# Five maxima over the partitions in a feed forward: by transpose and row maximum in place of a GpSimd reduction

## The chip, the cores and the metric

The kernel runs on one core of a Trainium2 chip. The metric is the device time of one execution in microseconds (us). PE is TensorE, DVE VectorE, ACT ScalarE, POOL GpSimd, SP SyncE, which issues most of the DMAs.

## The reference, cut to what matters

A decoder layer: self attention, cross attention, and a quantised feed forward, each followed by a layer norm. Four sequences of 1024 tokens are 4096 rows of 512. The change is in the feed forward:

```python
def act_qdq(x):
    scale = jnp.maximum(jnp.max(jnp.abs(x)) / qmax, 1e-12)     # one maximum over the whole tensor
    return jnp.clip(jnp.round(x / scale), -qmax - 1.0, qmax) * scale
x = act_qdq(x)
up = act_qdq(x @ lpbq_dequant(w_up).T)
gate = act_qdq(x @ lpbq_dequant(w_gate).T)
sig = fixed_qdq_u16(jax.nn.sigmoid(gate))
gate = act_qdq(gate * sig)
o = act_qdq(gate * up)
return o @ lpbq_dequant(w_down).T
```

Each `act_qdq` needs the largest absolute value of a whole tensor before one element of it can be rounded.

## The kernel before

The layer is a string of phases: preparation, self attention, projection, cross attention, and then the feed forward, which is `second_norm_phase`, `gate_phase`, `up_phase`, `product_phase` and `down_phase`. A phase is one block in which each engine has its own instruction stream, written out by hand with semaphores; a block ends when all engines have arrived and the last stores have landed, and then POOL clears the phase's semaphores and all engines meet again (`Kit.clear`). So no work of a phase begins before the one ahead of it is over on all engines.

- `second_norm_phase`: POOL adds (L1369), DVE normalises, ACT stores. DVE leaves in `pmax_x` a maximum for each partition.
- `gate_phase`: DVE rounds the input by `scale_x`, PE transposes it (L113) with the f32 identity `idf` and multiplies (L128), ACT evicts, DVE takes row maxima (L1550). POOL issues 26 DMAs of weights (L1524) and has nothing else.
- `up_phase`: PE multiplies 96 tiles of 128x512. For each ACT rounds the gate (`v_r`, L1648), takes the sigmoid (`v_s`, L1660) and evicts (L1669); POOL scales the sigmoid (`v_t`, L1693) and multiplies (`v_h`, L1682); DVE does the rest, among it `v_t` in place (L1724) and two row maxima.
- `product_phase`: 48 tiles of 128x1024 in rounds of four buffers. SP loads `j_h` (L1759) when DVE's product has freed the buffer; ACT rounds twice (L1801, L1804), POOL subtracts (L1813), DVE multiplies (L1828) and takes the row maximum (L1831). The first 24 tiles have their other factor and their result in SBUF (`rows`); the others load it and store the result.
- `down_phase`: ACT and DVE round and split, PE multiplies (L1927), DVE adds and normalises. POOL has nothing in it.

Between them stand the quantisers: `qx` (input), `qg` (gate), `quh` (up and h, two maxima) and the product's, which multiplies the maximum by a unit. Each is a block of its own. POOL reduces a 128x1 tile of maxima over the partitions (L1434, L1848), and DVE makes `scale` and `inverse` of it (L1440, L1442), which every partition needs. Nothing else runs in these blocks.

Of the kernel before, what the change touches and what calls it, by code (L numbers as in the profile page):

```python
# [15 lines left out]
F32 = mybir.dt.float32  # L16
# [3 lines left out]
ALU = mybir.AluOpType  # L20
ACT = mybir.ActivationFunctionType
AX = mybir.AxisListType
RMAX = bass.bass_isa.ReduceOp.max
ds = bass.ds

P = 128
# [1393 lines left out]
                dve.wait_ge(done, 1)  # L1420


def quantisers(nc, name, of):


    with ExitStack() as ctx:
        kit = Kit(nc, ctx)
        amax = [kit.sb(f"{name}_amax{j}", [P, 1], F32) for j in range(len(of))]
        reduced, steps = kit.sem(f"{name}_reduced"), kit.sem(f"{name}_steps")
        with nc.Block() as block:  # L1430
            @block.gpsimd
            def _(pool):
                for j, (pmax, scale, inverse) in enumerate(of):
                    nc.gpsimd.partition_all_reduce(amax[j][:], pmax[:], P, RMAX).then_inc(reduced, 1)  # L1434

            @block.vector
            def _(dve):
                for j, (pmax, scale, inverse) in enumerate(of):
                    dve.wait_ge(reduced, j + 1)
                    nc.vector.tensor_scalar(scale[:], amax[j][:], 1.0 / QMAX, 1e-12, ALU.mult, ALU.max).then_inc(steps, 1)  # L1440
                    dve.wait_ge(steps, 2 * j + 1)
                    nc.vector.reciprocal(inverse[:], scale[:]).then_inc(steps, 1)  # L1442
                    dve.wait_ge(steps, 2 * j + 2)
# [392 lines left out]
                dve.wait_ge(done, 1)  # L1836


def product_quantiser(nc, omax, sh, su, so, iso):

    with ExitStack() as ctx:
        kit = Kit(nc, ctx)
        amax, unit, inv = (kit.sb(f"qo_{n}", [P, 1], F32) for n in ("amax", "unit", "inv"))
        reduced, steps = kit.sem("qo_reduced"), kit.sem("qo_steps")
        with nc.Block() as block:
            @block.gpsimd
            def _(pool):
                nc.gpsimd.partition_all_reduce(amax[:], omax[:], P, RMAX).then_inc(reduced, 1)  # L1848

            @block.vector  # L1850
            def _(dve):
                nc.vector.tensor_tensor(unit[:], sh[:], su[:], ALU.mult).then_inc(steps, 1)
                dve.wait_ge(reduced, 1)
                dve.wait_ge(steps, 1)
                nc.vector.tensor_tensor(amax[:], amax[:], unit[:], ALU.mult).then_inc(steps, 1)
                dve.wait_ge(steps, 2)
                nc.vector.tensor_scalar(so[:], amax[:], 1.0 / QMAX, 1e-12, ALU.mult, ALU.max).then_inc(steps, 1)
                dve.wait_ge(steps, 3)
                nc.vector.reciprocal(inv[:], so[:]).then_inc(steps, 1)
                dve.wait_ge(steps, 4)  # L1860
                nc.vector.tensor_tensor(iso[:], inv[:], unit[:], ALU.mult).then_inc(steps, 1)
                dve.wait_ge(steps, 5)
# [125 lines left out]
def feed_forward(nc, c, attn2, x1_dram, w_dram, scratch, out):  # L1988

    x2_dram = scratch("scr_x2", [T, D], F32)  # L1990
    x_dram = [scratch(f"scr_xq_{n}", [NG, P, KT * GT], F16) for n in ("hi", "lo")]
    gate_dram, up_dram, h_dram, o_dram = (scratch(f"scr_{n}", [FT, P, T], F32) for n in ("gate", "up", "h", "o"))
    with ExitStack() as ctx:
        kit = Kit(nc, ctx)
        names = ("x", "gate", "up", "h", "o")
        pmax, scale, inverse = ({n: kit.sb(f"{k}_{n}", [P, 1], F32) for n in names} for k in ("pmax", "scale", "inverse"))
        of = lambda n: (pmax[n], scale[n], inverse[n])
        wd = [kit.sb(f"wd_{n}", [P, FT, D], F16) for n in ("hi", "lo")]

        res = kit.sb("rows", [P, RES * T], F32)  # L2000
        x2 = res[:, 0:T // P * D]
        with ExitStack() as up_scope:
            wu = [Kit(nc, up_scope).sb(f"wu_{n}", [P, FT, KT, P], F16) for n in ("hi", "lo")]
            with ExitStack() as gate_scope:
                wg = [Kit(nc, gate_scope).sb(f"wg_{n}", [P, FT, KT, P], F16) for n in ("hi", "lo")]
                tiles = lambda w, m: [(w[j][:].rearrange("p t k n -> p t (k n)"), w_dram[j][m * FT:(m + 1) * FT].rearrange("t p n -> p t n"))
                                      for j in range(2)]

                down_tiles = [(wd[j][:, k * KT:(k + 1) * KT, r * P:(r + 1) * P], w_dram[j][2 * FT + r * 3 + k].rearrange("p (q n) -> p q n", n=P))
                              for j in range(2) for r in range(KT) for k in range(3)]  # L2010
                second_norm_phase(nc, attn2, x1_dram, x2, x2_dram, pmax["x"], tiles(wg, 0))
                quantisers(nc, "qx", [of("x")])
                gate_phase(nc, c, x2, scale["x"], inverse["x"], wg, gate_dram, x_dram, pmax["gate"], tiles(wu, 1) + down_tiles)
            quantisers(nc, "qg", [of("gate")])
            up_phase(nc, x_dram, scale["x"], wu, gate_dram, scale["gate"], inverse["gate"], up_dram, res, h_dram,
                     pmax["up"], pmax["h"])
        quantisers(nc, "quh", [of("up"), of("h")])
        product_phase(nc, h_dram, up_dram, res, inverse["h"], inverse["up"], o_dram, pmax["o"])
        product_quantiser(nc, pmax["o"], scale["h"], scale["up"], scale["o"], inverse["o"])
        down_phase(nc, o_dram, res, scale["o"], inverse["o"], wd, x2_dram, out)  # L2020


def decoder_layer(nc, x, context, mask, Wq, bq, Wk, bk, Wv, bv, Wf, bf, w_gate, w_up, w_down, out):
    x = x.rearrange("b s d -> (b s) d")
    context = context.rearrange("b s d -> (b s) d")
    mask = mask.rearrange("b o q k -> (b o q) k")
    out = out.rearrange("b s d -> (b s) d")

    def scratch(name, shape, dt):
        return nc.dram_tensor(name, shape, dt).ap()  # L2030

    qk_dram = [scratch(f"scr_{n}", [B, D, S], F16) for n in ("q_hi", "q_lo", "k_hi", "k_lo")]
    q2_dram = [scratch(f"scr_q2_{n}", [B, D, S], F16) for n in ("hi", "lo")]
    k2_dram = [scratch(f"scr_k2_{n}", [B, D, S], F16) for n in ("hi", "lo")]
    v_dram, v2_dram = scratch("scr_v", [B * H, P, ST, VW], F16), scratch("scr_v2", [B * H, P, ST, VW], F16)
    mb_dram, nm_dram = scratch("scr_mb", [T, S], BF16), scratch("scr_nm", [B, S, S], F16)
    w_dram = [scratch(f"scr_w_{n}", [3 * FT, P, KT * P], F16) for n in ("hi", "lo")]
    place_dram = scratch("scr_place", [H, S], F16)
    attn, attn2, x1_dram = (scratch(n, [T, D], F32) for n in ("scr_attn", "scr_attn2", "scr_x1"))

    with ExitStack() as ctx:
        c = make_identities(nc, Kit(nc, ctx))
        preparation_phase(nc, c, x, Wq, bq, Wk, bk, Wv, bv, qk_dram, v_dram, context, k2_dram, v2_dram,
                          mask, mb_dram, nm_dram, (w_gate, w_up, w_down), w_dram)
        attention_phase(nc, c, "self", True, qk_dram[0:2], qk_dram[2:4], v_dram, attn, place_dram=place_dram)
        projection_phase(nc, c, attn, x, Wf, bf, x1_dram, q2_dram)
        attention_phase(nc, c, "cross", False, q2_dram, k2_dram, v2_dram, attn2, mb_dram, nm_dram)
        feed_forward(nc, c, attn2, x1_dram, w_dram, scratch, out)
# [21 lines left out]
```

## Time and profile before

| | us |
|---|---|
| median of 3 runs | 3291.91 (3290.72 to 3293.62) |
| the profiled execution, its own time | 3299.95 |
| its span | 3298.2 |

| engine | busy us | share of the span |
|---|---|---|
| PE | 2655.0 | 80% |
| DVE | 2426.0 | 74% |
| ACT | 1751.6 | 53% |
| POOL | 2008.6 | 61% |

The shares are means over phases with different limits. Times in the rows below are microseconds from the start of the span. An engine's idle time stands in brackets, with what ended it; "issue" means that the profile shows nothing that the engine waited for.

### The profile page before, as it was taken

The numbers are of one execution on the slowest core, as the hardware profiler recorded it, in microseconds if no ns is written. First come the engines' busy times: TensorE is split into PE (matmuls) and PEld (weight loads), VectorE is DVE, ScalarE is ACT, GpSimd is POOL, SyncE is SP. The second block draws the span as 40 slices with busy tenths as digits, with TensorE's granted clock in tenths as the row PEclk, the third lists the DMA queues.
The fourth block names the chain that finished last, engine by engine and source line by source line (L and its number), as shares of the span: only waits on it lengthen the run. The fifth ranks groups of instructions, "written<-read, shape, count | busy, mean of one in ns | idle before, by whom it ended". The sixth has DMA issues, their size and how long they took to land. (4 is left out here: it accounts for less than half of the span.)

```text
span 3298.2 us, 79323 instructions
## 1 busy us (share of the span) xinstructions
PE 2655.0 (80%) x24114; PEld 1432.6 (43%) x24114; DVE 2426.0 (74%) x4633; ACT 1751.6 (53%) x3234; POOL 2008.6 (61%) x1479
## 2 busy tenths in 40 slices
PE   6888748888886969999999999904998899301999
PEld 3444325555553525555555555502444333100444
DVE  7778757777774777888888888765433899785776
ACT  2433327777775526666666666601332666585333
POOL 2334369999997309999999999943000566441000
PEclk9999969999998979999999999956999999755999
DMA  7999934444445651131131221176333677587332
GB/s 242 298 304 289 308 101 130 136 131 129 131 140 179 231 189 36 46 96 51 43 98 45 66 81 48 48 270 207 137 119 146 205 249 244 184 307 303 122 121 83
DMA packets 339452, 518.73 MB, mean 157 GB/s; under 512 B 36165, under 2 KB 169029, under 8 KB 339354
## 3 DMA queue, kind: packets, MB, share of 16 engines
q1 hardware_dynamic: 331066, 499.72, 47.4%
q0 software_dynamic: 2752, 9.44, 0.9%
q10 hardware_dynamic: 5536, 8.40, 0.7%
q8 instruction: 45, 0.74, 0.1%
q14 instruction: 53, 0.43, 0.0%
HBM read 278.56 MB, written 202.67 MB: 146 GB/s over the span
## 5 line engine op out<-in xcount | busy, mean ns | idle before, releaser
L1085 POOL TENSOR_TENSOR cross_plo<-cross_p 128x1024 f16<-128x1024 f32 x448 | 906.4, 2056 | 73.8 <-ACT cross_p L923 69.7
L923 ACT ACTIVATE cross_p<-cross_st 128x512 f32<-128x512 f32 x1024 | 556.1, 595 | 289.3 <-PE cross_st L857 289.3
L998 DVE CUSTOM_DVE_ANT_0 cross_junk<-cross_sc,cross_mb 128x1024 bf16<-128x1024 f32 x512 | 619.3, 1220 | 110.1 <-PE cross_sc L818 98.3
L1085 POOL TENSOR_TENSOR self_plo<-self_p 128x1024 f16<-128x1024 f32 (+7 forms) x512 | 576.7, 1161 | 20.4 <-ACT self_p L923 20.1
L923 ACT ACTIVATE self_p<-self_st,self_strip 128x512 f32<-128x512 f32 (+3 forms) x768 | 415.3, 582 | 149.1 <-PE self_st L855 118.2
L998 DVE CUSTOM_DVE_ANT_0 self_junk<-self_sc,self_strip 128x1024 bf16<-128x1024 f32 (+7 forms) x512 | 371.3, 753 | 141.9 <-PE self_sc L818 136.0
L852 PE MATMUL cross_st<-cross_qa,cross_ka 97*128 97x512 f16 x1024 | 390.6, 381 | 2.3 <-ACT cross_p L923 1.9
L857 PE MATMUL cross_st<-cross_nm,idbig 128*128 128x512 f16 x1024 | 390.0, 381 | 0.0
L818 PE MATMUL cross_sc<-cross_ka,cross_qa 96*128 96x512 f16 x1024 | 311.3, 386 | 21.9 <-DMA cross_ka<-scr_k_hi 16.6
L1927 PE MATMUL d_acc<-wd_hi,d_oh 128*128 128x512 f16 x384 | 146.7, 382 | 204.4 <-DVE d_ol L1965 204.4
L880 PEld LDWEIGHTS cross_o<-cross_vh,cross_p 128*128 128x128 bf16 x4096 | 270.1, 97 | 75.1 <-issue 21.8
L880 PE MATMUL cross_o<-cross_vh,cross_p 128*128 128x65 f16 x4096 | 297.4, 191 | 4.7 <-POOL cross_plo L1085 4.3
L881 PE MATMUL cross_o<-cross_vh,cross_plo 128*128 128x33 f16 x4096 | 291.1, 179 | 0.0
L852 PE MATMUL self_st<-self_qa,self_ka 98*128 98x512 f16 (+3 forms) x768 | 244.4, 334 | 48.7 <-ACT self_p L923 44.2
L881 PEld LDWEIGHTS cross_o<-cross_vh,cross_plo 128*128 128x128 f16 x4096 | 249.1, 96 | 53.9
L818 PE MATMUL self_sc<-self_ka,self_qa 96*128 96x512 f16 (+3 forms) x768 | 212.8, 334 | 53.9 <-DVE self_strips L972 27.9
L880 PE MATMUL self_o<-self_vh,self_p 128*128 128x65 f16 x2304 | 199.2, 192 | 40.4 <-DVE self_osum L1021 19.9
L510 POOL TENSOR_TENSOR qk_out<-y,qk_out 128x512 f16<-128x512 f32 x64 | 74.1, 1158 | 203.0 <-DVE qk_out L475 203.0
L880 PEld LDWEIGHTS self_o<-self_vh,self_p 128*128 128x128 bf16 x2304 | 163.1, 98 | 74.9 <-issue 43.6
L881 PE MATMUL self_o<-self_vh,self_plo 128*128 128x33 f16 x2304 | 191.8, 179 | 0.0
L1550 DVE TENSOR_REDUCE gt_tmax<-gt_y 128x512 f32 x96 | 65.8, 685 | 162.1 <-ACT gt_y L1515 162.1
L128 PE MATMUL v_acc<-v_xh,wu_hi 128*128 128x512 f16 x384 | 148.9, 388 | 33.9 <-ACT rows L1669 21.7
(241 smaller groups left out, 6007.2 us busy)
## 6 DMA issues: line engine op xcount, KB each, us to landing
self_strip<-self_strips SPq DMA_DIRECT2D x68, 516.0 KB, 3.2
v_g<-scr_gate SPq DMA_DIRECT2D x97, 256.0 KB, 3.8
scr_gate<-gt_y SPq DMA_DIRECT2D x96, 256.0 KB, 2.0
scr_h<-v_h SPq DMA_DIRECT2D x96, 256.0 KB, 2.4
j_h<-scr_h SPq DMA_DIRECT2D x48, 512.0 KB, 6.0
m<-in_mask_Bx1xSxS_ik SPq DMA_DIRECT2D x34, 512.0 KB, 7.6
d_o<-scr_o SPq DMA_DIRECT2D x9, 1536.0 KB
scr_up<-v_y SPq DMA_DIRECT2D x48, 256.0 KB, 3.5
```

Of the source, the lines that this page charges most:

```text
L128: mm = nc.tensor.matmul(out, a, b, start=(n == 0), stop=(n == len(terms) - 1))
L510: nc.gpsimd.tensor_tensor(qk[:, n // 4, 1, n % 4], y32[:, n % 4], qk[:, n // 4, 0, n % 4], ALU.subtract).then_inc(l_done, 1)
L818: mm = nc.tensor.matmul(sc[slot % 2][:, k - k0:k - k0 + w], qa[j][0:3 * HD, qt * P:(qt + 1) * P], ka[j][0:3 * HD, k:k + w], start=True, st ...
L852: mm = nc.tensor.matmul(out[:, 0:w], lhs, qa[j][0:KR, q0:q1], start=True, stop=causal)
L857: mm = nc.tensor.matmul(out[:, 0:w], c["idbig"][:], nm[kt][:, q0:q1], start=False, stop=True)
L880: nc.tensor.matmul(out[:, qt % 4, :], high[:, q], vh[n % NQK][:, kt, :], start=first, stop=False, skip_group_check=True)
L881: mm = nc.tensor.matmul(out[:, qt % 4, 0:HD + 1], plo[u % NPR][:, q], vh[n % NQK][:, kt, 0:HD + 1], start=False, stop=last_kt, skip_group_ ...
L923: nc.scalar.activation(p32[u % NPR][:, q0:q1], stp[cc % 2][:, 0:q1 - q0], ACT.Exp, bias=bias, scale=SM).then_inc(expd, 1)
L998: nc.vector.tensor_tensor_reduce(junk[slot % 2][:, 0:w], sc[slot % 2][:, 0:w], bias, 1.0, -3e38, ALU.add, ALU.max, qmax[n % 2][:, qt:qt + ...
L1085: nc.gpsimd.tensor_tensor(plo[u % NPR][:, q], p32[u % NPR][:, q], high[:, q], ALU.subtract).then_inc(lo_g, 1)
L1550: nc.vector.tensor_reduce(tmax[:, ds(g * FT + o, 1)], y[o % NY][:], AX.X, ALU.max, apply_absolute_value=True).then_inc(maxed, 1)
L1927: mm = nc.tensor.matmul(acc[tt % 2][:], a[:, k, t], b[:, k, :], start=(n == 0), stop=(n == 3 * FT - 1))
```

## The change

The reduction on POOL is replaced by three steps. DVE copies the 128x1 maxima over 128 columns (`wide`), PE transposes that tile into PSUM (`turned`), so that each partition has all 128 maxima in its row, and DVE takes the maximum of the row. In `quh` the two copies are issued first, and then reduction and scale of one tensor after the other.

```diff
-def quantisers(nc, name, of):
+def quantisers(nc, c, name, of):
     with ExitStack() as ctx:
         kit = Kit(nc, ctx)
+        wide = [kit.sb(f"{name}_wide{j}", [P, P], F32) for j in range(len(of))]
         amax = [kit.sb(f"{name}_amax{j}", [P, 1], F32) for j in range(len(of))]
-        reduced, steps = kit.sem(f"{name}_reduced"), kit.sem(f"{name}_steps")
+        turned = [kit.ps(f"{name}_t{j}", [P, P]) for j in range(len(of))]
+        spread, across, reduced, steps = (kit.sem(f"{name}_{n}") for n in ("spread", "across", "reduced", "steps"))
         with nc.Block() as block:
-            @block.gpsimd
-            def _(pool):
-                for j, (pmax, scale, inverse) in enumerate(of):
-                    nc.gpsimd.partition_all_reduce(amax[j][:], pmax[:], P, RMAX).then_inc(reduced, 1)
+            @block.tensor
+            def _(pe):
+                for j in range(len(of)):
+                    pe.wait_ge(spread, j + 1)
+                    nc.tensor.transpose(turned[j][:], wide[j][:], c["idf"][:]).then_inc(across, 1)
             @block.vector
             def _(dve):
                 for j, (pmax, scale, inverse) in enumerate(of):
+                    nc.vector.tensor_copy(wide[j][:], pmax[:].to_broadcast([P, P])).then_inc(spread, 1)
+                for j, (pmax, scale, inverse) in enumerate(of):
+                    dve.wait_ge(across, j + 1)
+                    nc.vector.tensor_reduce(amax[j][:], turned[j][:], AX.X, ALU.max).then_inc(reduced, 1)
                     dve.wait_ge(reduced, j + 1)
                     nc.vector.tensor_scalar(scale[:], amax[j][:], 1.0 / QMAX, 1e-12, ALU.mult, ALU.max).then_inc(steps, 1)
...
-def product_quantiser(nc, omax, sh, su, so, iso):
+def product_quantiser(nc, c, omax, sh, su, so, iso):
...
         with nc.Block() as block:
-            @block.gpsimd
-            def _(pool):
-                nc.gpsimd.partition_all_reduce(amax[:], omax[:], P, RMAX).then_inc(reduced, 1)
+            @block.tensor
+            def _(pe):
+                pe.wait_ge(spread, 1)
+                nc.tensor.transpose(turned[:], wide[:], c["idf"][:]).then_inc(across, 1)
             @block.vector
             def _(dve):
+                nc.vector.tensor_copy(wide[:], omax[:].to_broadcast([P, P])).then_inc(spread, 1)
                 nc.vector.tensor_tensor(unit[:], sh[:], su[:], ALU.mult).then_inc(steps, 1)
+                dve.wait_ge(across, 1)
+                nc.vector.tensor_reduce(amax[:], turned[:], AX.X, ALU.max).then_inc(reduced, 1)
                 dve.wait_ge(reduced, 1)
```

## Rows read from the trace of the kernel before

**Rows 1.** The page's first line.
```profile
span 3298.2 us, 79323 instructions
```
**Rows 2.** Busy time in stretches: up phase, product phase's first and second half.
```profile
core 0: us, PE busy (x) PEld busy (x) DVE busy (x) ACT busy (x) POOL busy (x), PEclk, DMA share, GB/s
2640.00:2840.00 200.00, 181.30 (x807) 77.18 (x804) 187.53 (x273) 137.74 (x211) 136.43 (x138) 0.98 0.74 247
2900.00:2920.00 20.00, 0.00 (x0) 0.00 (x0) 19.47 (x18) 19.19 (x17) 9.12 (x8) 0.50 0.68 215
2940.00:2980.00 40.00, 0.00 (x0) 0.00 (x0) 26.38 (x22) 25.86 (x21) 11.30 (x11) 0.50 1.03 419
```
**Rows 3.** Timeline, product quantiser: start, us, engine, line, operation, idle before.
```profile
3021.33 0.16 DVE L1852 TENSOR_TENSOR qo_unit<-scale_h,scale_up 128x1 f32<-128x1 f32 x1 [2.10 <-PEq L58]
3027.29 0.38 POOL L1848 PARTITION_ALL_REDUCE qo_amax<-pmax_o  x1 [10.91 <-issue]
3027.70 0.16 DVE L1855 TENSOR_TENSOR qo_amax<-qo_amax,qo_unit 128x1 f32<-128x1 f32 x1 [6.21 <-POOL qo_amax L1848]
```
**Rows 4.** The line of the product's last store, its start and time to landing.
```profile
L1775 SPq DMA_DIRECT2D scr_o<-j_o x1: 332/332/332, 3017.7 to 3017.7; - x1
...
DMA to landing us min/median/max: 2.6/2.6/2.6
```
**Rows 5.** The same of the gate's last store.
```profile
L1480 SPq DMA_DIRECT2D scr_gate<-gt_y x1: 332/332/332, 2540.8 to 2540.8; - x1
...
DMA to landing us min/median/max: 2.1/2.1/2.1
```
**Rows 6.** Timeline, the quantiser behind the gate phase.
```profile
2544.30 0.35 POOL L1434 PARTITION_ALL_REDUCE qg_amax<-pmax_gate  x1 [255.37 <-ACTq L1430]
2544.68 0.15 DVE L1440 TENSOR_SCALAR scale_gate<-qg_amax 128x1 f32<-128x1 f32 x1 [2.92 <-POOL qg_amax L1434]
```
**Rows 7.** Timeline of ACT, POOL and DVE, beginning of the up phase.
```profile
2558.78 0.63 ACT L1660 ACTIVATE v_s<-v_q 128x512 f32<-128x512 f32 x1
...
2566.39 1.20 POOL L1693 TENSOR_SCALAR v_t<-v_s 128x512 f32<-128x512 f32 x2 [21.74 <-issue]
...
2567.03 0.84 DVE L1724 TENSOR_SCALAR v_t<-v_t 128x512 f32<-128x512 f32 x1 [9.04 <-POOL v_t L1693]
```
**Rows 8.** Timeline of ACT and POOL, beginning of the product phase.
```profile
2862.27 1.22 ACT L1804 ACTIVATE rows<-rows,j_magic,inverse_up 128x1024 f32<-128x1024 f32 x1
...
2870.78 5.04 POOL L1813 TENSOR_SCALAR rows<-rows 128x1024 f32<-128x1024 f32 x4 [14.86 <-ACT rows L1804]
...
2877.50 1.24 ACT L1801 ACTIVATE j_h<-j_h,j_magic,inverse_h 128x1024 f32<-128x1024 f32 x1 [7.21 <-DMA j_h<-scr_h]
```
**Rows 9.** Timeline of POOL, projection phase.
```profile
1060.67 0.80 POOL L1206 PARTITION_BROADCAST bf_all<-bf_row  x1 [17.02 <-DMA bf_row<-in_L_attn_bf]
1069.01 1.25 POOL L1212 TENSOR_TENSOR px<-px,bf_all 128x512 f32<-128x512 f32 x1 [7.54 <-issue]
```
**Rows 10.** The page's costliest groups: count, busy us, mean ns, idle before.
```profile
L1550 DVE TENSOR_REDUCE gt_tmax<-gt_y 128x512 f32 x96 | 65.8, 685 | 162.1 <-ACT gt_y L1515 162.1
```
**Rows 11.** The gate phase's first f32 transposes, by line (min/median/max ns) and in the timeline.
```profile
L113 PE MATMUL gate_t<-idf,gt_xq x16: 421/421/476, 2269.4 to 2273.5; 128*128 128x128 f32 x16
...
2269.45 1.97 PE L113 MATMUL gate_t<-idf,gt_xq 128*128 128x128 f32 x8 [115.91 <-DVE gt_xq L1538]
...
2270.60 0.59 ACT L118 CAST gt_xh<-gate_t 128x512 f16<-128x512 f32 x1 [20.24 <-PE gate_t L113]
```
**Rows 12.** Timeline of POOL, the quantiser behind the second norm.
```profile
2264.48 0.38 POOL L1434 PARTITION_ALL_REDUCE qx_amax<-pmax_x  x1 [18.68 <-issue]
```
**Rows 13.** Timeline of POOL and DVE, the quantiser of up and h.
```profile
2855.20 0.38 POOL L1434 PARTITION_ALL_REDUCE quh_amax<-pmax_up  x1 [8.87 <-issue]
...
2855.61 0.15 DVE L1440 TENSOR_SCALAR scale_up<-quh_amax 128x1 f32<-128x1 f32 x1 [7.93 <-POOL quh_amax L1434]
...
2856.22 0.16 DVE L1442 RECIPROCAL inverse_h<-scale_h 128x1 f32<-128x1 f32 x1
```

More of the change, by code:

```diff
@@ L1836, in _ @@
                 dve.wait_ge(done, 1)
-def product_quantiser(nc, omax, sh, su, so, iso):
+def product_quantiser(nc, c, omax, sh, su, so, iso):
     with ExitStack() as ctx:
         kit = Kit(nc, ctx)
+        wide, turned = kit.sb("qo_wide", [P, P], F32), kit.ps("qo_t", [P, P])
         amax, unit, inv = (kit.sb(f"qo_{n}", [P, 1], F32) for n in ("amax", "unit", "inv"))
-        reduced, steps = kit.sem("qo_reduced"), kit.sem("qo_steps")
+        spread, across, reduced, steps = (kit.sem(f"qo_{n}") for n in ("spread", "across", "reduced", "steps"))
         with nc.Block() as block:
-            @block.gpsimd
-            def _(pool):
-                nc.gpsimd.partition_all_reduce(amax[:], omax[:], P, RMAX).then_inc(reduced, 1)
+            @block.tensor
+            def _(pe):
+                pe.wait_ge(spread, 1)
+                nc.tensor.transpose(turned[:], wide[:], c["idf"][:]).then_inc(across, 1)
             @block.vector
             def _(dve):
+                nc.vector.tensor_copy(wide[:], omax[:].to_broadcast([P, P])).then_inc(spread, 1)
                 nc.vector.tensor_tensor(unit[:], sh[:], su[:], ALU.mult).then_inc(steps, 1)
+                dve.wait_ge(across, 1)
+                nc.vector.tensor_reduce(amax[:], turned[:], AX.X, ALU.max).then_inc(reduced, 1)
                 dve.wait_ge(reduced, 1)
@@ L2011, in feed_forward @@
                 second_norm_phase(nc, attn2, x1_dram, x2, x2_dram, pmax["x"], tiles(wg, 0))
-                quantisers(nc, "qx", [of("x")])
+                quantisers(nc, c, "qx", [of("x")])
                 gate_phase(nc, c, x2, scale["x"], inverse["x"], wg, gate_dram, x_dram, pmax["gate"], tiles(wu, 1) + down_tiles)
-            quantisers(nc, "qg", [of("gate")])
+            quantisers(nc, c, "qg", [of("gate")])
             up_phase(nc, x_dram, scale["x"], wu, gate_dram, scale["gate"], inverse["gate"], up_dram, res, h_dram,
                      pmax["up"], pmax["h"])
-        quantisers(nc, "quh", [of("up"), of("h")])
+        quantisers(nc, c, "quh", [of("up"), of("h")])
         product_phase(nc, h_dram, up_dram, res, inverse["h"], inverse["up"], o_dram, pmax["o"])
-        product_quantiser(nc, pmax["o"], scale["h"], scale["up"], scale["o"], inverse["o"])
+        product_quantiser(nc, c, pmax["o"], scale["h"], scale["up"], scale["o"], inverse["o"])
         down_phase(nc, o_dram, res, scale["o"], inverse["o"], wd, x2_dram, out)
```

## The prediction

> **What bounds the kernel now.** I read the page first. The execution lasts 3298.2 us of span [rows 1], 3299.95 us as that execution was timed; what lies around the span is 1.75 us. The busy shares of the whole say little here, because the kernel is a string of phases and each ends in a barrier over all engines. So I went to the table of stretches next: one stretch of the up phase and two of the product phase, which stand behind quantisers [rows 2]. The reader is to see that a different thing is the limit in each. In the up phase DVE is busy 187.53 of 200 us. In the product phase it is DVE at first (19.47 of 20 us) and then the DMA engines (share 1.03, 419 GB/s). In neither is it POOL. But between two phases nothing runs, and whatever the quantiser there takes is added to the end, in full.
>
> Then the timeline of those gaps, an engine at a time. The product quantiser shows its whole inside, because DVE has an instruction at once when the block opens: `qo_unit` starts at 3021.33, the reduction on POOL at 3027.29, and DVE goes on at 3027.70 [rows 3]. The reduction itself lasts 0.38 us. The 5.96 us before it are idle, with "issue" as their reason: POOL waited for nothing that the profile shows. What it waited for isn't the store before the barrier either: the last one was issued at 3017.7 and took 2.6 us, so it had landed at 3020.3, 1.0 us before the block opened [rows 4].
>
> In the quantiser behind the gate phase the same instruction has no such wait. The last store before it was issued at 2540.8 and took 2.1 us [rows 5]; with the same 1.0 us of barriers the block opens at about 2543.9, and the reduction starts at 2544.30, 0.4 us later [rows 6]. What sets it apart is what POOL did before: in the gate phase only DMA issues, in the other phases elementwise work. Behind each reduction there is the counterpart. POOL's first elementwise instruction of the up phase needs `v_s`, which ACT ended at 2558.78 + 0.63 = 2559.41, and starts at 2566.39, and the page's reason for its idle time is "issue" again [rows 7]. In the product phase POOL's input was ready at 2862.27 + 1.22 = 2863.49 and it started at 2870.78 [rows 8]. The same is seen far from here, where a partition broadcast ends at 1061.47 and the next addition is 7.54 us later, "issue" [rows 9]. I read this as a change of POOL's program: some 6 us to go from elementwise work to a partition operation, some 7 us to come back, and nothing when it stays on one side.
>
> So the cost of the five reductions isn't the 0.4 us each that their bars show. It is three ways there and two ways back (after the first POOL stays where it is until the second, and after the last it has nothing more to do).
>
> **The change part by part.** Removed: five reductions on POOL. Added, for each: a copy on DVE that spreads the 128x1 maxima over 128x128, a transpose on PE, a reduction over the row on DVE out of PSUM; and more semaphores and one PSUM tile for each. The trace has no such copy and no 128x128 row reduction, so I take them between two rows: DVE's 128x1 operation takes 0.15 us [rows 6] and its 128x512 f32 reduction 0.685 us [rows 10]; 128 columns on that line come to 0.15 + 0.53 x 127/511 = 0.29 us, for both. Bounds: 0.15 and 0.69 us. For the transpose the nearest rows are the f32 transposes with the same identity that begin the gate phase, on a PE that had stood idle: 0.42 to 0.48 us each, while four in a row, from the start at 2269.45 to ACT's start on the result at 2270.60, took 1.15 us [rows 11]. I take 0.48 and keep 0.42 and 1.15 as bounds. A hand-over between engines is 0.03 us (reduction over at 2544.65, DVE at 2544.68 [rows 6]); there are three. The chain from the opening of a block to the maximum is then 0.29 + 0.48 + 0.29 + 0.09 = 1.15 us, with bounds 0.15 + 0.42 + 0.15 + 0.09 = 0.8 and 0.69 + 1.15 + 0.69 + 0.09 = 2.6 us.
>
> *Product quantiser:* from block opening to DVE going on it was 3027.70 - 3021.33 = 6.37 us; now 1.15. Gain 5.2. `qo_unit` moves under the transpose.
>
> *Quantiser behind the second norm:* its reduction starts at 2264.48, and its wait is booked "issue" too [rows 12]. The opening isn't marked by any instruction; I take the same 6.37 us. Gain 5.2.
>
> *Quantiser of up and h:* opening at 2855.20 - 5.96 = 2849.24, last reciprocal over at 2856.22 + 0.16 = 2856.38 [rows 13], 7.14 us. The new chain: 1.15 to the first maximum, 0.77 for the two pairs of scale and inverse as now (2855.61 to 2856.38), and 0.32 for the second row reduction and its hand-over, which was hidden before and now stands between the pairs on DVE: 2.24. The second copy runs under the first transpose and the second transpose under the first reduction. Gain 4.9.
>
> *Quantiser behind the gate:* from about 2543.9 to 2544.68 it was 0.8 us, now 1.15. Loss 0.35.
>
> Sum of the quantisers: 5.2 + 5.2 + 4.9 - 0.35 = 15.0 us.
>
> *Way back in the up phase:* POOL starts at 2559.44 and not at 2566.39: 6.95 us. DVE stood idle for 9.04 us until that result [rows 7] and is the phase's limit afterwards [rows 2], so it can't be hidden there. PE, the next one, has room for it at 181.30 of 200 us. I take all of it; the other end is nothing, if PE or the loads should set the pace at the start.
>
> *Way back in the product phase:* POOL starts at 2863.52 and not at 2870.78: 7.26 us. ACT had all four tiles of the first round ready and then stood 7.21 us until the reload of the first buffer landed at 2877.50 [rows 8]; that reload is issued only when DVE's product has freed the buffer, which waits for POOL. So the loads move forward too. The DMA-bound half of the phase has a fixed amount to move, and begins when the first half ends; DVE at 19.47 of 20 us carries the shift through the first half. I take all of it; the other end is nothing.
>
> Sum of both: 14.2 us, and with the quantisers 29.2 us. The profiled execution would be 3299.95 - 29.2 = 3270.8 us. The median before is 8.0 us below that execution, so I take the difference from the median: 3291.9 - 29.2 = 3262.7 us.
>
> What costs nothing: the extra semaphores are cleared with the others between phases, and the gap is the same 1.0 us behind the product phase with its many semaphores [rows 3, 4]; if each did cost something it would be hundredths. PE and its identity are free in every gap. POOL's DMA issues in the gate phase need no change of program: they follow the opening. Neither does the clock of PE matter: in the up and product phases PE is not the limit, and the gate and down phases begin after a long idle as before.
>
> The page speaks for one part and against another. In the Trainium skill, GPSIMD Engine Reference, Instruction dispatch, the first call to a freshly loaded kernel pays for loading it, about 6 us (5.95 us), with no visible instruction in the profile. The row at 5.96 us [rows 3] agrees. The page prices the way there only; by it alone the two ways back would have another cause and stay, and the result would be the first rival below. The same page's Engine selection says that a reduction along the partitions is GPSIMD's work, by which this change would be the wrong way round; for a single column these rows say the reverse.
>
> **Rivals.** (1) *Only the ways there go.* The two late starts of elementwise work in the up and product phases belong to POOL's first instruction of a phase, and stay. Gain 15.0 us, 3276.9. For it: both are the first of their phase, after idle times of 21.74 and 14.86 us [rows 7, 8]. Against: the case at 1069.01 has the 7.5 us in the middle of a phase, right behind a partition operation [rows 9].
>
> (2) *The product phase swallows its part.* If the DMA engines set its end by something that doesn't begin earlier, the 7.26 us are lost and the gain is 21.9: 3270.0. For it: a share of 1.03 in the second half [rows 2]. Against: the loads hang on DVE's products from the start.
>
> (3) *The other side: PE inherits the wait.* The idle 6 us could be the price of the first instruction of any engine in a new block after a long idle. PE would then pay it in the quantisers, and POOL would go on paying it in the two phases. Each chain is 1.15 + 6.0 = 7.15 us: 0.8 more than before in three places and 6.35 more in the fourth, 8.8 us in all, 3300.7. If POOL's ways back do vanish, it ends on the slower side only from 8.5 us per chain. Against: PE began the gate phase's transposes after 116 us of idle with no such delay, and its wait is booked to DVE [rows 11].
>
> **How the numbers follow.** The forecast has 0.80, the first rival 0.07, the second 0.08, the third 0.03, anything else 0.02. The forecast's own bounds: the four chains between 0.8 and 2.6 us give 1.4 us more or 6.2 us less gain (the second row reduction of one of them included), the ways back were measured once each and may differ by a us or two together. That is 3261 to 3269, with a spread of the median of some 1.5 us on both sides. The range reaches a little below, and above over the second rival: 3258 to 3274. It leaves out the first and third and a little, about 1 in 8. A measurement of this kernel can tell about 0.2%, 6.6 us, from no change: the forecast, the first two rivals and most of the rest are faster by more than that, 0.96; within it 0.02; the third 0.02 to 0.03, slower 0.02.
>
> **What the profile afterwards would show.** No partition reduction behind 2200 us. In the product quantiser, from `qo_unit` or the copy to the product with the unit, about 1.2 us and not 6.4. POOL's first elementwise operation in the up and product phases within 0.1 us of ACT's result, and DVE's idle before its first `v_t` some 2 us, not 9. In the product phase ACT goes on from the first round to the second with no wait of 7 us. The down phase only begins earlier. I am wrong if "issue" waits stay at POOL's first operations, if PE's transpose starts more than 0.1 us after the copy, or if the product phase ends no earlier relative to its first load.

## The result and the profile after

| | before | after |
|---|---|---|
| median, us | 3292.76 (3290.72 to 3301.03, 4 runs) | 3251.3 (3248.11 to 3253.57, 4 runs) |
| ratio | | 0.9868 [0.9853, 0.9884] |
| the profiled execution, us | 3299.95 | 3251.63 |

The change gains 41.5 us by the medians. The forecast was 29.2 us, and 3251.3 lies below its range. The two profiled executions differ by 48.3 us; that of before lies 7.2 us above the median of its kernel.

The page of the changed kernel, its first line and the busy time of the engines:

```profile
span 3249.8 us, 79322 instructions
PE 2651.1 (82%) x24119; PEld 1432.6 (44%) x24119; DVE 2429.3 (75%) x4643; ACT 1748.9 (54%) x3234; POOL 2016.7 (62%) x1474
```

Against [rows 1] the span is 48.4 us shorter, and each engine's busy time is within 9 us of what it was. No work went away; idle time did.

**The quantisers.** The timeline of the changed kernel, behind the second norm, where the prediction's chain stands alone:

```profile
2243.30 0.23 DVE L1442 COPY qx_wide<-pmax_x 128x128 f32<-128x128 f32 x1 [3.20 <-PEq L58]
2243.59 0.47 PE L1437 MATMUL qx_t<-idf,qx_wide 128*128 128x128 f32 x1 [105.44 <-DVE qx_wide L1442]
2244.10 0.29 DVE L1445 TENSOR_REDUCE qx_amax<-qx_t 128x1 f32<-128x128 f32 x1 [0.57 <-PE qx_t L1437]
2244.42 0.15 DVE L1447 TENSOR_SCALAR scale_x<-qx_amax 128x1 f32<-128x1 f32 x1
```

Copy 0.23 us, transpose 0.47 on a PE that had stood for 105 us, row maximum 0.29: 1.12 us from the opening to the first use, where the reduction on POOL had its 5.96 us of "issue" and 0.38 of work [rows 3]. The same timeline in the quantiser of up and h (its first copy and its last reciprocal) and in the product's:

```profile
2820.20 0.23 DVE L1442 COPY quh_wide<-pmax_up 128x128 f32<-128x128 f32 x1 [1.88 <-PEq L58]
...
2822.22 0.17 DVE L1449 RECIPROCAL inverse_h<-scale_h 128x1 f32<-128x1 f32 x1
...
2978.35 0.23 DVE L1861 COPY qo_wide<-pmax_o 128x128 f32<-128x128 f32 x1 [2.11 <-PEq L58]
...
2979.47 0.16 DVE L1867 TENSOR_TENSOR qo_amax<-qo_amax,qo_unit 128x1 f32<-128x1 f32 x1
```

That is 2822.39 - 2820.20 = 2.19 us and 2979.47 - 2978.35 = 1.12 us.

**The ways back.** The timeline of the changed kernel at the beginning of the up phase, and of ACT and POOL at that of the product phase:

```profile
2537.38 0.63 ACT L1667 ACTIVATE v_s<-v_q 128x512 f32<-128x512 f32 x1
...
2538.24 0.62 POOL L1700 TENSOR_SCALAR v_t<-v_s 128x512 f32<-128x512 f32 x1 [269.72 <-ACT v_s L1667]
...
2538.89 0.43 DVE L1731 TENSOR_SCALAR v_t<-v_t 128x512 f32<-128x512 f32 x1 [2.31 <-POOL v_t L1700]
...
2828.28 1.23 ACT L1811 ACTIVATE rows<-rows,j_magic,inverse_up 128x1024 f32<-128x1024 f32 x1
2829.70 1.04 POOL L1820 TENSOR_SCALAR rows<-rows 128x1024 f32<-128x1024 f32 x1 [12.74 <-ACT rows L1811]
...
2836.20 1.23 ACT L1808 ACTIVATE j_h<-j_h,j_magic,inverse_h 128x1024 f32<-128x1024 f32 x1
```

POOL's idle time now ends with ACT, not with "issue" as in [rows 7, 8]. It starts 2538.24 - 2538.01 = 0.23 us and 2829.70 - 2829.51 = 0.19 us behind ACT's result, and ACT goes from the first round of the product phase to the second without the 7.21 us of before.

**A place that the prediction didn't look at** is the first ten microseconds. POOL and SP at the start, in the timeline of the kernel before:

```profile
1.01 0.20 POOL L82 MEMSET idbig<- 128x128 f16 x1
...
8.33 0.28 POOL L85 TENSOR_SCALAR_AFFINE_SELECT idf<-idf 128x128 f32<-128x128 f32 x1 [7.11 <-issue]
...
9.58 1.81 SPq L241 DMA_DIRECT2D w_q<-in_L_attn_Wq  x4
```

and in that of the changed kernel:

```profile
1.01 0.20 POOL L82 MEMSET idbig<- 128x128 f16 x1
1.47 0.28 POOL L85 TENSOR_SCALAR_AFFINE_SELECT idf<-idf 128x128 f32<-128x128 f32 x1 [0.25 <-POOL idbig L82]
...
2.73 1.80 SPq L241 DMA_DIRECT2D w_q<-in_L_attn_Wq  x4
```

Nothing of this code was changed. The select waited 7.11 us for "issue" and waits no more, and everything behind it, SP's first load too, is 6.9 us earlier. The selects build the identities, and the first block ends with them.

The two profiles side by side, as the time that lies between the same two points of each:

| part | forecast | measured |
|---|---|---|
| quantiser behind the second norm | 5.2 | 5.1 |
| quantiser behind the gate | -0.35 | -0.8 |
| quantiser of up and h | 4.9 | 4.6 |
| product quantiser | 5.2 | 5.2 |
| way back, up phase | 6.95 | 6.75 |
| way back, product phase | 7.26 | 7.1 |
| sum | 29.2 | 28.0 |
| start of the execution | none | 6.9 |
| product phase beyond its late start | none | 1.9 in this pair, up to 10 in others |

The last row is the stretch from ACT's first `j_h` to the reduction `pmax_o`: 157.9 us before and 148.9 after, 9.0 shorter, of which the late start is 7.1. What then remains of the 48.3 us between the profiles, 11.5 us, is in phases that have neither a changed instruction nor a change of POOL's program at their end. By the timeline the last addition of the preparation starts 13.1 us earlier (404.4 and 391.3), 6.2 more than the start gives. The later profiles put that down to scatter between executions and chips: from the first select to this addition it is 396.1 and 391.0 us in two profiles of before, and 389.8, 397.9 and 391.3 us in three of after. Neither kernel has the shorter one throughout.

### The profile page after: what moved, and what is told of

Its sections match the earlier page's. It is cut to its first block and busy times, and to the rows that moved or that the text cites. A ratio compares the mean times of both kernels' runs of the same rounds, so it can differ in the third digit from the quotient of the medians.

```text
span 3249.8 us, 79322 instructions
## 1 busy us (share of the span) xinstructions
PE 2651.1 (82%) x24119; PEld 1432.6 (44%) x24119; DVE 2429.3 (75%) x4643; ACT 1748.9 (54%) x3234; POOL 2016.7 (62%) x1474
## 5 line engine op out<-in xcount | busy, mean ns | idle before, releaser
L857 PE MATMUL cross_st<-cross_nm,idbig 128*128 128x512 f16 x1024 | 389.8, 381 | 0.0
L1700 POOL TENSOR_SCALAR v_t<-v_s 128x512 f32<-128x512 f32 x96 | 59.9, 624 | 356.2 <-ACT v_s L1667 349.4
```

Of the source, the lines that this page charges most:

```text
L857: mm = nc.tensor.matmul(out[:, 0:w], c["idbig"][:], nm[kt][:, q0:q1], start=False, stop=True)
```

## The experiments

My theory after the result: POOL's program stays loaded from one execution to the next, so the last reduction of one leaves the way back to the first select of the next. And in the product phase a late POOL costs more than its delay, because it meets DVE in another order. The rival for the start: it belongs to chance or to the state of the chip, and for the product phase: the delay alone counts and the rest is scatter.

**The kernel after, again, on one chip with the next three.**

> The changed kernel once more, as it is. The profile before it and its first profile differ by 48.3 us of time, 34.6 us of which lie in places that the prediction has terms for or that the start shows (28.0 in quantisers and ways back, 6.9 at POOL's first affine select, which starts at 1.47 and not at 8.33 us), and some 8 us in the preparation and attention phases, where no instruction was changed. If those 8 us are scatter from one execution to the next, they differ between two profiles of one kernel, the ratio of medians is 0.987 to 0.989, and the profile of this run has its last addition of the preparation (404.4 us before, 391.3 after) anywhere between 391 and 398 us. If they belong to the change, it comes at 391 again.

3267.58 us (3263.49 to 3271.03) beside 3309.2 for before: 0.9877 [0.9862, 0.9892], 41 us again. The last addition of the preparation starts at 399.4 us, later than either side of the expectation had it.

**A reduction given back at the end**, on POOL in the down phase, where it has nothing else, on a tile of its own (this and the idle operations below leave out nothing of the computation):

```diff
+            @block.gpsimd
+            def _(pool):
+                nc.gpsimd.memset(idle_a[:], 1.0).then_inc(idle_done, 1)
+                pool.wait_ge(idle_done, 1)
+                nc.gpsimd.partition_all_reduce(idle_b[:], idle_a[:], P, RMAX).then_inc(idle_done, 1)
...
```

> The changed kernel, with one partition reduction of a tile of ones on POOL at the beginning of the down phase, where POOL has nothing else; its result is used by nothing. Theory: the program that POOL holds at the end of an execution is still there when the next one begins; the kernel before ended with the partition operations and so had to change back at its first affine select, behind which all engines wait. Then POOL's idle time before that select is about 7 us again and the kernel is 6 to 7.5 us slower than the changed one, some 34 to 36 us faster than before, with nothing else moved. Rival: the early start at 1.47 us comes from something else in the changed program (its layout, its number of semaphores). Then the select stays at 1.5 us and the time is that of the changed kernel within 1 us.

3273.46 us (3267.81 to 3278.39), 5.9 more than the kernel after. The times of the two overlap (after goes up to 3271.03), so this difference alone isn't clear of noise; the timeline at the start is what decides:

```profile
8.43 0.28 POOL L85 TENSOR_SCALAR_AFFINE_SELECT idf<-idf 128x128 f32<-128x128 f32 x1 [7.21 <-issue]
```

An operation 3 ms further down, hidden under the down phase, has put 7 us at the front. Nothing ahead of it differs from the kernel after, so what the select finds is what the execution before has left.

**The reverse: the kernel before, with a 128x1 scaling at the end.**

```diff
...
+                nc.gpsimd.tensor_scalar(idle_b[:], idle_a[:], 2.0, 1.0, ALU.mult, ALU.add).then_inc(idle_done, 1)
...
```

> The kernel before, with its five reductions on POOL, and one 128x1 scaling on POOL at the beginning of the down phase, used by nothing. If what POOL holds at the end is carried over to the next execution, this change back to elementwise work is hidden under the down phase, the select at the start comes at about 1.5 us and not 8.3, and the kernel is 6 to 7.5 us faster than before (ratio 0.998). If it isn't carried over, the time is that of before.

3299.19 us, 0.9968 [0.9955, 0.998]: by the ratio a gain of 10.6 us (6.6 to 14.9) by one idle instruction. The timeline:

```profile
1.72 0.29 POOL L85 TENSOR_SCALAR_AFFINE_SELECT idf<-idf 128x128 f32<-128x128 f32 x1 [0.50 <-POOL idbig L82]
```

The select is 6.6 us earlier than 8.33, which is the lower end of the interval. The rival gave no gain here; it falls. Why the time gained more than the select isn't shown; scatter would do.

**The kernel before, with the new product quantiser alone** (its reduction was the last partition operation of the execution).

> The kernel before with only the product quantiser in its new form. Its reduction is gone: by the prediction's terms 5.2 us. It has no way back of its own. But the last thing POOL did is then elementwise work of the product phase: if that is carried over, the start gives 6.9 us more, 12.1 us in all (ratio 0.9963). Without it 5.2 us (0.9984).

3298.92 us, 0.9965 [0.9952, 0.9977]. Its select starts at 1.72 us too. So giving up this one reduction was worth 10.3 to 11.6 us (by the medians and by the ratio, whose interval is 7.6 to 15.9) and not 5.2. The parts are read in the profiles: 6.6 us at the start, and 5.2 in its place, where `pmax_o` to `inverse_o` takes 4.0 us and in the run before this one 9.2. The times don't separate them: the two runs are 0.3 us apart, since in the profile of this one the product phase ended 5.2 us later for no reason that the change gives.

**The order in the product phase.** First the shape of the thing. One line for each kernel's POOL and DVE operations on the resident tiles `rows` (least, median and largest ns; first and last start). The profiled execution of before:

```profile
L1813 POOL TENSOR_SCALAR rows<-rows x24: 1034/1194/2138, 2870.8 to 2927.7; 128x1024 f32<-128x1024 f32 x24
L1828 DVE SCALAR_TENSOR_TENSOR rows<-j_h,rows x24: 1212/1216/2059, 2871.9 to 2929.0; 128x1024 f32<-128x1024 f32 x24
```

of after:

```profile
L1820 POOL TENSOR_SCALAR rows<-rows x24: 1044/1625/2062, 2829.7 to 2884.5; 128x1024 f32<-128x1024 f32 x24
L1835 DVE SCALAR_TENSOR_TENSOR rows<-j_h,rows x24: 1212/1216/2078, 2830.8 to 2887.8; 128x1024 f32<-128x1024 f32 x24
```

and of before in its second profile:

```profile
L1813 POOL TENSOR_SCALAR rows<-rows x24: 1037/1047/2007, 2863.5 to 2926.2; 128x1024 f32<-128x1024 f32 x24
L1828 DVE SCALAR_TENSOR_TENSOR rows<-j_h,rows x24: 1216/1702/2059, 2864.6 to 2929.5; 128x1024 f32<-128x1024 f32 x24
```

By the medians, either POOL's operation is stretched and DVE's product takes its 1.22 us, or POOL's takes its 1.04 and DVE's product is stretched; the largest values show that a profile can hold some of both. Which it is can be seen in the timeline. The second profile of before, where POOL starts first:

```profile
2887.14 1.05 POOL L1813 TENSOR_SCALAR rows<-rows 128x1024 f32<-128x1024 f32 x1 [1.85 <-ACT rows L1804]
...
2887.53 1.73 DVE L1828 SCALAR_TENSOR_TENSOR rows<-j_h,rows 128x1024 f32<-128x1024 f32 x1
```

and the kernel after, where DVE does:

```profile
2857.04 1.22 DVE L1835 SCALAR_TENSOR_TENSOR rows<-j_h,rows 128x1024 f32<-128x1024 f32 x1
2857.22 1.94 POOL L1820 TENSOR_SCALAR rows<-rows 128x1024 f32<-128x1024 f32 x1 [0.45 <-ACT rows L1811]
```

The one that comes second pays, and about what is left of the first: DVE's product ends 1.07 us after POOL's end at 2888.19, and POOL's operation 0.90 us after DVE's end at 2858.26, as if each had begun only then. POOL has room for it and DVE, the limit, has not. From the first to the last start on POOL the 24 tiles take 2926.2 - 2863.5 = 62.7 us in the one order and 2884.5 - 2829.7 = 54.8 in the other. The profiled execution of before fell into the dear order only for its first tiles and took 56.9. Its stretched products:

```profile
2871.85 2.06 DVE L1828 SCALAR_TENSOR_TENSOR rows<-j_h,rows 128x1024 f32<-128x1024 f32 x1 [14.44 <-POOL rows L1813]
...
2875.08 1.81 DVE L1828 SCALAR_TENSOR_TENSOR rows<-j_h,rows 128x1024 f32<-128x1024 f32 x1
...
2880.45 1.73 DVE L1828 SCALAR_TENSOR_TENSOR rows<-j_h,rows 128x1024 f32<-128x1024 f32 x1
```

That is 5.60 - 3 x 1.22 = 1.94 us, the 1.9 us of the table.

In the Trainium skill, GPSIMD Engine Reference, Specifications, GPSIMD shares its SBUF interfaces with VectorE and collides with DVE instructions that have two SBUF inputs. The product is such an instruction and the rows agree (1.22 and 1.73 us).

A busy share hides it. Twenty microseconds of the first half in the table of stretches, the second profile of before:

```profile
core 0: us, PE busy (x) PEld busy (x) DVE busy (x) ACT busy (x) POOL busy (x), PEclk, DMA share, GB/s
2892.00:2912.00 20.00, 0.00 (x0) 0.00 (x0) 19.76 (x15) 17.15 (x15) 7.43 (x8) 0.50 0.61 187
```

and a later profile of after:

```profile
2840.00:2860.00 20.00, 0.00 (x0) 0.00 (x0) 19.73 (x18) 19.48 (x18) 9.64 (x8) 0.50 0.69 217
```

DVE is busy for 19.7 us in both, and does 15 instructions in the one and 18 in the other.

> The kernel before once more, as it is, for the scatter of its profile. The stretch from ACT's first work on j_h to the end of the last maximum of the product phase took 157.9 us in the first profile of this kernel, 164.0 and 165.5 us in the two profiles of kernels that still change POOL's program in that phase, and 147.8 to 148.9 us in the three that don't. If the 157.9 is the rule, the other two were disturbed by something else; if it scatters within one kernel, it lies anywhere between 155 and 166 here.

3299.64 us; it is the second profile of before shown above, with a product stretch of 164.9 us.

**POOL late, without any change of program.** The kernel after, where POOL waits in the product phase until its first input is there and then scales a tile of its own seven times:

```diff
...
+                pool.wait_ge(added, 2)
+                for n in range(7):
+                    pool.wait_ge(late_done, n + 1)
+                    nc.gpsimd.tensor_scalar(late[:], late[:], 1.0, 0.0, ALU.mult, ALU.add).then_inc(late_done, 1)
...
```

> The changed kernel, where POOL in the product phase waits for ACT's first pair of results and then does seven scalings of a 128x1024 tile of its own, used by nothing, some 7.5 us, before it begins with the real tiles. No change of program takes place. First theory, delay alone: 7 to 8 us slower than the changed kernel. Second theory, delay and order: as in the kernels with the way back, the median of DVE's product rises above 1.22 us, the stretch from ACT's first work to the last maximum comes to 157 us or more, and it is 9 to 17 us slower than the changed kernel. Third: if the extra time needs the change of program itself, the stretch is 155 to 156 us.

3270.83 us, 0.991 [0.9895, 0.9925]; the kernel after stood at 0.9877 on another chip, 0.0033 or 11 us lower. Each ratio is uncertain by some 0.0015, so the times alone don't tell 11 us from the 7 to 8 of the delay; the stretch does. The timeline:

```profile
2835.24 7.80 POOL L1822 TENSOR_SCALAR late<-late 128x1024 f32<-128x1024 f32 x7 [5.46 <-ACT rows L1812]
```

and by line:

```profile
L1827 POOL TENSOR_SCALAR rows<-rows x24: 1039/1044/2009, 2843.3 to 2905.6; 128x1024 f32<-128x1024 f32 x24
L1842 DVE SCALAR_TENSOR_TENSOR rows<-j_h,rows x24: 1215/1649/2045, 2844.3 to 2908.9; 128x1024 f32<-128x1024 f32 x24
```

Seven scalings, 7.80 us behind the first input, gave a stretch of 164.7 us, 16 more than after's 148.9 in the profiles and 11 by the medians, with the product at a median of 1649 ns. The delay accounts for 7.8 of the 16. A late POOL is enough to bring the dear order; it needs no change of program.

**The order alone.** The kernel before, where POOL starts a resident tile only when DVE has made the product of the one before it. POOL starts as late as ever:

```diff
                     pool.wait_ge(added, (f * TR + j) * 2 + 2)
+                    if resident:
+                        pool.wait_ge(prod, f * TR + j)
```

> The kernel before, its reductions and all changes of program on POOL as they are; in the first half of the product phase POOL waits, before each of the 24 tiles, until DVE's product of the tile before is done. It then works under DVE's row maximum and not under its product. If it is the order in which the two meet that costs time behind the late start, DVE's product returns to 1.22 us and the stretch from POOL's first tile to its 24th falls from 62 to 64 us (56.9 in one profile) to 55 to 57: 5 to 8 us faster than before, ratio 0.9975 to 0.9985, though POOL starts as late as ever. If the stretch is long because of the loads (ACT waits for them as well), it stays at 62 us or grows, and the time is that of before or worse.

3292.22 us, 0.9981 [0.9972, 0.999] (one execution of 7066 us is left out), 6.1 us less than before by the medians, 3 to 9 by the interval. The lines of `rows`:

```profile
L1815 POOL TENSOR_SCALAR rows<-rows x24: 1034/1045/1046, 2867.0 to 2924.4; 128x1024 f32<-128x1024 f32 x24
L1830 DVE SCALAR_TENSOR_TENSOR rows<-j_h,rows x24: 1224/1225/1226, 2868.1 to 2925.5; 128x1024 f32<-128x1024 f32 x24
```

Two tiles in its timeline:

```profile
2889.22 1.22 DVE L1833 TENSOR_REDUCE j_tmax<-rows 128x1 f32<-128x1024 f32 x1
2889.36 1.04 POOL L1815 TENSOR_SCALAR rows<-rows 128x1024 f32<-128x1024 f32 x1 [1.44 <-DVE rows L1830]
...
2890.44 1.23 DVE L1830 SCALAR_TENSOR_TENSOR rows<-j_h,rows 128x1024 f32<-128x1024 f32 x1
```

POOL works under DVE's row maximum, nobody is stretched, and the 24 tiles take 57.4 us: less than the 62.7 of the second profile of before, not less than the 56.9 of the first. A wait more made the kernel faster. So the order costs some 6 us on the average of before's executions.

**The way back ahead of the first tile.** The kernel before, with an idle scaling at the head of POOL's product stream, so that the program changes while the first loads are under way:

```diff
...
+                nc.gpsimd.tensor_scalar(idle_b[:], idle_a[:], 2.0, 1.0, ALU.mult, ALU.add).then_inc(idle_done, 1)
...
```

> The kernel before, with one 128x1 scaling by POOL as the first thing of the product phase, used by nothing: the way back to elementwise work then begins when the block opens and not when ACT's first result is there, and is over at about the time at which that result comes. All reductions stay on POOL. First theory, the prediction's: the way back costs its delay alone, 7.3 us less what is left over, some 6.5 us (ratio 0.998). Second theory: the late start also sets the order in which POOL and DVE meet in the first half, POOL first, and DVE's product is then stretched from 1.22 to 1.5 to 2.06 us, 2 to 9 us over 24 tiles. Then the stretch from ACT's first work to the last maximum falls to 148 to 150 us, DVE's product has a median of 1.22 us, and the gain is 9 to 16 us (ratio 0.995 to 0.997).

3295.82 us, 0.9988 [0.9979, 0.9998]: below both theories, with the first one's 0.998 at the edge of the interval. The lines of the configuration instructions, by line:

```profile
L1813 POOLq MODIFY_POOL_CONFIG  x2: 11/11/11, 2850.8 to 2850.9; - x2
```

and in its timeline:

```profile
2860.83 0.18 POOL L1813 TENSOR_SCALAR pr_idle_b<-pr_idle_a 128x1 f32<-128x1 f32 x1 [10.01 <-issue]
2861.22 5.04 POOL L1818 TENSOR_SCALAR rows<-rows 128x1024 f32<-128x1024 f32 x4 [0.21 <-POOL pr_idle_b L1813]
```

The change took 10.0 us, not the 7.1 to 7.3 of the quiet places. POOL gained 3.1 us on its start, not 7, and the order wasn't mended (product median 1489 ns). As a test of the order it tells nothing, since POOL still came late. What it shows instead is that the change is not of a fixed length: it is longer beside the loads of `j_h`. The other runs bear it out. The table of stretches for the change back in before's product phase and for the one at the start of the down phase in the run with the scaling at the end (columns as in the table above):

```profile
2863.80:2870.80 7.00, 0.00 (x0) 0.00 (x0) 0.00 (x0) 6.48 (x6) 0.01 (x1) 0.50 0.05 21
3029.80:3040.00 10.20, 0.98 (x3) 0.28 (x3) 2.28 (x7) 2.93 (x4) 0.03 (x1) 0.50 0.93 316
```

With the DMA engines at a share of 0.05 it takes 7 us, at 0.93 it takes 10.26 us. The way there is longer too: the idle reduction at the start of the down phase waited 8.96 us and not 5.96. In front of an operation that may need a change stand two configuration instructions on POOL's queue. They are no sign of a wait by themselves: both kernels have them ahead of the first select, at 1.4 us, and only before waits. In the Trainium skill, GPSIMD Engine Reference, Instruction dispatch, that instruction can bring in new code by DMA. A load that competes for the DMA engines would fit the 9 to 10 us; no run here shows its packets.

**Every change early, no reduction removed.** The kernel before, with idle reductions at the end of POOL's work in the second norm, up and product phases and idle scalings at the start of up, product and down:

> The kernel before with all five reductions on POOL, but each change of program started by an idle operation where POOL has nothing to do: a reduction at the end of its work in the second norm, up and product phases, a scaling at the beginning of the up, product and down phases. If the gain of the change is the price of these changes of program and not of the reduction, this kernel gets nearly all of it: start 6.9, second norm 5.5, up and h 2.9 (POOL ends late there), product 4.8, ways back 6.9 and 6.5, and the order in the product phase 2 to 9, in all 35 to 42 us, ratio 0.987 to 0.990. If the transposes themselves bring something, it stays above the changed kernel by more than 6 us.

3270.84 us, 0.9907 [0.9891, 0.9922]: 30 us of the gain (26 to 36) with all five reductions still on POOL. By the medians it falls short of the 35 us expected. Behind the second norm the reduction with its program already there is as good as the new chain: 3.8 us from maximum to scale, against 9.4 before and 4.3 after. In the quantiser of up and h little is gained, since POOL ends the up phase late and the change there holds up the barrier: 8.0 us from the last maximum to the start of the last reciprocal, against 8.5 before and 3.9 after. And in the product phase POOL still came late enough: first input to first tile 6.8 us, not 9.7, and the dear order, 62.6 us for the 24 tiles. So some three quarters of what the change gives come without a single transpose, by moving the changes of POOL's program out of the way.

**The kernel after, a third time, and the quantisers without blocks of their own.** The last kernel issues the same copies, transposes and maxima at the head of the next phase's PE and DVE streams, so that the phase's loads go out first:

```diff
-    quantisers(nc, c, "qx", [of("x")])
...
+        on_pe, on_dve = quantiser_streams(nc, c, kit, "qx", quantise_first)
...
             def _(pe):
+                on_pe(pe)
...
             def _(dve):
+                on_dve(dve)
```

> The changed kernel as it is, beside the two others of this call: ratio to before 0.987 to 0.988, DVE's product in the first half of the product phase with a median of 1.22 us.

> The changed kernel without blocks of their own for the quantisers: their instructions stand at the head of PE's and DVE's streams of the phase behind. One barrier with clearing is gone in four places (1.05 to 1.1 us each), and in the up, product and down phases SP issues its first loads when the block opens, with the quantiser's chain (1.5, 2.2 and 1.9 us) under them; in the gate phase only the barrier is saved, since DVE's first work needs the scale. 1.1 + 2.6 + 3.2 + 3.0 = 10 us faster than the changed kernel, ratio to before 0.984 to 0.985. Rival: the first loads are not what the phases wait for; then 4.3 us. POOL's order in the product phase should stay as in the changed kernel.

3256.42 us (0.9879 [0.9864, 0.9895]) for the kernel after and 3246.75 us (0.9843 [0.983, 0.9856]) for the merged one, beside 3298.32 for before. The merged one is 9.7 us faster by the medians, the fastest kernel here. Its timeline at the start of the product phase:

```profile
2818.45 1.77 SPq L1770 DMA_DIRECT2D j_h<-scr_h  x4
2818.49 0.23 DVE L1437 COPY quh_wide<-pmax_up 128x128 f32<-128x128 f32 x1 [1.92 <-PEq L58]
...
2820.51 0.16 DVE L1444 RECIPROCAL inverse_h<-scale_h 128x1 f32<-128x1 f32 x1
...
2822.47 1.24 ACT L1812 ACTIVATE j_h<-j_h,j_magic,inverse_h 128x1024 f32<-128x1024 f32 x1 [10.67 <-DMA j_h<-scr_h]
```

The quantiser is over at 2820.67, and the tile that it is for lands at 2822.47. Here it costs nothing, and the barrier and clearing of its own block are gone with it. In the gate phase DVE's first work needs the scale, so the chain itself isn't hidden there.

## Why the prediction was right, and where not

- **The gap between phases is added in full, and "issue" is a change of POOL's program, 6 us there and 7 us back.** Right. Four quantisers: 14.1 us measured, 15.0 forecast; in up and h I had put the opening 0.3 us too early. Two ways back: 13.9 measured, 14.2 forecast. The chain took 1.12 us, the estimate was 1.15.
- **The quantiser behind the gate loses 0.35.** It lost 0.8, the largest error among the chains. Its opening before was an estimate from a store, and too early: in the kernel after, DVE begins 2.61 us behind the last maximum of the gate phase, and before, the reduction began 2.54 us behind the same point, so it stood right at the opening and not 0.4 us behind it.
- **Rival 1, the ways back stay.** Refuted: POOL starts 0.2 us behind ACT's result in both phases (I had said within 0.1), and DVE's idle time before its first `v_t` is 2.31 us (I had said some 2). **Rival 2, the product phase swallows its part.** Refuted: it gave back all of it and more. **Rival 3, PE inherits the wait.** Refuted: PE starts 0.06 us after the copy's end, on an engine idle for 105 us.
- **The step that failed is the count of the ways back:** "It is three ways there and two ways back (after the first POOL stays where it is until the second, and after the last it has nothing more to do)." There is a third, at the first select of the next execution. It is worth 6.9 us in the profiles, 5.9 and 10.6 us in the two runs that set it alone, the first not clear of noise, the last with an interval that begins at 6.6. With it the forecast would have been 3255.8 us: the missing term is larger than the room that the range left below. The row that says so was in the trace of before: a select that waits 7.11 us for "issue" in a kernel that has done nothing yet. By the prediction's own reading of "issue", POOL there had to come from a partition operation, and the only one was that of the execution before. I had gone through the phases around the change and not through all of POOL's "issue" waits.
- **The mis-sized term is the way back in the product phase.** The forecast was 7.26 us, with the argument that "DVE at 19.47 of 20 us carries the shift through the first half". It does carry the shift. But I looked at one stretch, in which each product takes its 1.22 us, and not at the first tiles, where three products are stretched by 1.9 us in all, nor could this one profile show that other executions are stretched through the whole half. The whole term is 9.0 us between the two profiles and 157.9 to 164.9 less 147.6 to 148.9 = 9 to 17 us over all of them. The order's share of it was measured alone at 6.1 us (3 to 9).

The account: 28.0 us of the forecast's terms, 6.9 at the start, 2 to 10 from the order, 37 to 45 us; measured 41.5, and 41.6 and 41.9 in the two repetitions. With the 6.1 us of the order run it is 41.0. That the sum fits so well is partly luck: each gain has some us of uncertainty.

**What stays open.** Why before's executions fall into the dear order for the whole of the phase in one profile and for a part in another; the runs show that a late start brings it and that an order by hand removes it, not where it tips. And the 5 to 8 us by which the preparation differs between profiles of one kernel, which no run here went into.

## What to carry to other kernels

List every wait of POOL that ends with "issue", from the first microsecond on, and give each an owner. A partition operation among elementwise work costs a change of program there and one back, 6 and 7 us here and 9 and 10 beside heavy loads, whatever the operation itself lasts, and the last one of an execution is paid at the start of the next. If the operation has to stay, let an idle one bring the program in while POOL has nothing to do, which helps as far as POOL's idle time reaches; if it is a maximum of one column, transpose it and put the chain at the head of the next phase, under its loads.

Where DVE is the limit and POOL works beside it on SBUF, look at the durations and not at the busy share, and let POOL start second: one wait was worth 6 us (3 to 9).

## What the runs showed of the hardware that was not expected

- What POOL has loaded outlives the execution: the select at 1.47 or at 8.33 us, by the last POOL operation of the kernel alone.
- The change back took 9.5 to 10.3 us beside a stream of loads (DMA share 0.59 to 0.93) and 7.0 to 7.3 us in quiet places (share 0.00 to 0.05); the way there 8.96 and 5.96 us.
- When a POOL operation and a DVE instruction with two SBUF inputs overlap, the one that starts second is stretched: DVE's from 1.22 to 1.73 us (up to 2.06), or POOL's from 1.04 to 1.94.
